# Attention of a gated block computed in two halves of 256 tokens through a state, and the zero rows stored later at the start

## The reference

```python
log_f = jax.nn.log_sigmoid(fg)
pcs = jnp.pad(jnp.cumsum(log_f, axis=-1), ((0, 0), (0, 0), (1, 0)))
mat = pcs[..., :, None] - pcs[..., None, :]
log_fg_matrix = jnp.where(ltr, mat[..., 1:, 1:], -jnp.inf)
log_D = log_fg_matrix + ig[..., None, :]
max_log_D = jnp.max(log_D, axis=-1, keepdims=True)
D = jnp.exp(log_D - max_log_D)
C = jnp.einsum('bhsd,bhtd->bhst', qh, kh) / math.sqrt(dh) * D
normalizer = jnp.maximum(jnp.abs(C.sum(axis=-1, keepdims=True)), jnp.exp(-max_log_D))
hst = jnp.einsum('bhst,bhtd->bhsd', C / (normalizer + eps), vh)
# heads normalised and scaled; x = x + tanh(g) * heads; then the experts on the normalised x
```

## Time and profile of the kernel before

| | us |
|---|---|
| median of three runs (lowest, highest) | 1904.91 (1904.54, 1905.46) |
| the profiled execution | 1903.81 |
| its span | 1902.1 |
| TensorE busy in the span | 1808.4 (95%) |
| VectorE busy | 1279.3 (67%) |
| ScalarE busy | 1100.7 (58%) |
| GpSimd busy | 689.4 (36%) |

### The profile page before, as it was taken

One profiled execution on the slowest core, in us unless ns is written; L12 is line 12 of the kernel. 1 busy time (PEld: TensorE's weight loads), 2 busy tenths in 40 slices (PEclk: granted clock), 3 DMA queues, 4 the chain that ended last, 5 costly groups with the idle time before them and its releaser, 6 DMA issues.

```text
span 1902.1 us, 29803 instructions
## 1 busy us (share of the span) xinstructions
PE 1808.4 (95%) x11068; PEld 1568.3 (82%) x11068; DVE 1279.3 (67%) x2890; ACT 1100.7 (58%) x2022; POOL 689.4 (36%) x507
## 2 busy tenths in 40 slices
PE   5999986699999999999999999999999999999997
PEld 3777765688888888888888888888888888888886
DVE  3799978786657665766576657665766576667551
ACT  3668667665555555555655565556555655565542
POOL 1101110425343533353435333533353435343333
PEclk8999987699999999999999999999999999999999
DMA  5364624525555555555555555555555555555544
GB/s 187 99 224 175 210 101 126 135 54 112 98 117 100 109 100 115 102 109 101 112 103 110 100 112 102 113 97 113 102 113 98 112 102 112 100 111 93 96 74 58
DMA packets 177777, 214.41 MB, mean 113 GB/s; under 512 B 20464, under 2 KB 102512, under 8 KB 176608
## 3 DMA queue, kind: packets, MB, share of 16 engines
q0 software_dynamic: 50176, 90.77, 31.4%
q1 hardware_dynamic: 127456, 121.74, 20.5%
HBM read 123.10 MB, written 89.34 MB: 112 GB/s over the span
## 4 chain that ended last, share of the span: by engine, by line
PE 85%; DVE 8%; ACT 3%; issue 2%; DMA 1%; SPq 1%; POOL 1%; POOLq 0%; DVEq 0%; ACTq 0%
PE PS L964 41%; PE PS L942 35%; PE PS L791 2%; PE PS L920 2%; PE PS L782 2%; DVE stats L1356 1%; PE PS L810 1%; DVE decay L1413 1%; PE PS L730 1%; DVE x_lo L1701 1%; DVE stats L1425 1%; DVE xn L1365 1%; DVE x_back L1468 1%; PE PS L744 1%; DVE heads L1463 1%
## 5 line engine op out<-in xcount | busy, mean ns | idle before, releaser
L644 POOL DMA_INDIRECT out_dram<-y_out,rows_now x288 | 484.0, 1681 | 813.0 <-ACT y_out L1272 734.8
L942 PE MATMUL PS<-x_hi,w_hi 128*128 128x270 f32 x1792 | 520.0, 290 | 6.2 <-DVE x_lo L1701 4.3
L942 PE MATMUL PS<-x_lo,w_hi 128*128 128x270 f32 x1792 | 516.5, 288 | 0.0
L942 PE MATMUL PS<-x_hi,w_lo 128*128 128x270 f32 x1792 | 516.2, 288 | 0.0
L964 PE MATMUL PS<-w_hi,h_hi 128*120 128x512 f32 x1152 | 458.0, 398 | 6.7 <-DVE h_lo L1708 6.7
L964 PE MATMUL PS<-w_lo,h_hi 128*120 128x512 f32 x1152 | 453.8, 394 | 0.0
L964 PE MATMUL PS<-w_hi,h_lo 128*120 128x512 f32 x1152 | 453.2, 393 | 0.0
L942 PEld LDWEIGHTS PS<-x_hi,w_hi 128*128 128x128 f32 x1792 | 339.3, 189 | 31.2 <-issue 4.6
L942 PEld LDWEIGHTS PS<-x_lo,w_hi 128*128 128x128 f32 x1792 | 340.2, 190 | 21.0
L942 PEld LDWEIGHTS PS<-x_hi,w_lo 128*128 128x128 f32 x1792 | 339.0, 189 | 0.0
L964 PEld LDWEIGHTS PS<-w_hi,h_lo 128*120 128x120 f32 x1152 | 208.9, 181 | 58.8
(11 more groups left out here) (194 smaller groups left out, 2283.2 us busy)
## 6 DMA issues: line engine op xcount, KB each, us to landing
w_raw<-in_L_ffn_W_dram SPq DMA_DIRECT2D x128, 256.0 KB, 4.0
w_raw<-in_L_ffn_W_dram SPq DMA_DIRECT2D x64, 512.0 KB, 4.5
x_front<-in_x_dram SPq DMA_DIRECT2D x8, 1024.0 KB, 7.0
vs<-in_ctx_dram SPq DMA_DIRECT2D x32, 256.0 KB, 4.9
maxima<-maxima_rows SPq DMA_DIRECT2D x8, 1024.0 KB, 4.6
x_back<-in_x_dram SPq DMA_DIRECT2D x8, 1024.0 KB, 8.8
out_dram<-x_back SPq DMA_DIRECT2D x8, 1024.0 KB, 6.8
xn_rows<-xn SPq DMA_DIRECT2D x8, 1024.0 KB, 7.5
```

The source lines that it names most:

```text
L644: G.indirect_dma_start(out=out[:, :], out_offset=bass.IndirectOffsetOnAxis(ap=rows_now[0:RT, u % HI:u % HI + 1], axis=0), in_=y_out[0:RT, ...
L942: ins = T.matmul(product_at(k, i), w[:, slot, a, kt * P:(kt + 1) * P], v[:, side, x, kt, :], start=(kt == 0 and n == 0), stop=(kt == 1 and ...
```

## The change

A batch is attended in two halves of 256 tokens. Inside a half it is as before: keys of the half, decay, mask, scores, weighing (block pairs of both halves in one instruction, 512 columns for the even and 256 for the odd key blocks). What the second half reads of the first goes through a state of 128 x 129 for each head: the values of the first half are weighed by exp(col[t] - max[255]) (`weight_logs` on VectorE, `exp_weights` on ScalarE, `weigh_values` on GpSimd), TensorE sums the products of keys and weighed values (`states`, two heads a call), ScalarE copies them (`copy_state`). The queries of the second half are faded by exp(max[255] - max[s]) (`exp_fade` on ScalarE, `fade_queries` on GpSimd) and multiplied with the state in `outputs`. Context is key and value at once, so the state needs no turned copy. On SyncE, `slot(-1)` is put before the stores of the zero rows. The core of the diff (semaphores and buffers left out):

```diff
@@ sync @@
             load_ctx(1)
+            slot(-1)
             sp.dma_start(xn_dram[TOK:TOK + P, :], zeros[:, :]).then_inc(xn_stored, 16)
...
-            for b in range(-1, B):
+            for b in range(0, B):
                 slot(b)
@@ gpsimd @@
+            def weigh_values(b):
+                pool.wait_ge(front_copied, at(b, 8, 8))
+                pool.wait_ge(w_made, at(b, 1, 1))
+                wait_past(pool, state_made, at(b, 2, 0))
+                for t in range(2):
+                    each = w_first[:, t, :].rearrange("p (h o) -> p h o", o=1).to_broadcast([P, NH, VW])
+                    ins = G.tensor_tensor(v_first[:, t, :, :], vs[b % CTX_BUFS][:, t, :, :], each, ALU.mult)
+                ins.then_inc(v_weighed, 1)
+            def fade_queries(b, r):
+                pool.wait_ge(fade_made, at(b, 2, r + 1))
+                wait_past(pool, head_summed, at(b, 4, 0))
+                mine = slice(2 * r, 2 * r + 2)
+                G.tensor_tensor(q_faded[:, mine, :], qT[b % 2][:, mine, HALF:S], fade[:, mine, :], ALU.mult).then_inc(q_scaled, 1)
             def slot(b):
-                if there(b):
-                    for h in range(NH):
-                        mask(b, h)
+                mask(b, 0)
+                weigh_values(b)
+                fade_queries(b, 0)
+                mask(b, 1)
+                mask(b, 2)
+                fade_queries(b, 1)
+                mask(b, 3)
@@ tensor @@
-                for place, t in enumerate(SCORE_ORDER):
-                    wait_past(pe, scored, at(b, 16, 4 * h + READ[place]))
-                    T.matmul(score_ps[t], kT[p][:, h, t * P:(t + 1) * P], qT[p][:, h, t * P:S],
-                             start=True, stop=True).then_inc(scores_made, 1)
+                for v in range(2):
+                    wait_past(pe, scored, at(b, 2 * NH, 2 * h + v - 1))
+                    for u in range(2):
+                        t = 2 * u + v
+                        ins = T.matmul(score_ps[v][:, u, :], kT[p][:, h, t * P:(t + 1) * P], qT[p][:, h, t * P:(u + 1) * HALF],
+                                       start=True, stop=True)
+                    ins.then_inc(scores_made, 1)
+            def states(b, r):
+                pe.wait_ge(v_weighed, at(b, 1, 1))
+                wait_past(pe, state_copied, at(b, 2, r))
+                for i in range(2):
+                    h = 2 * r + i
+                    for t in range(2):
+                        ins = T.matmul(state_ps[:, i, :], vs[b % CTX_BUFS][:, t, h, 0:DH], v_first[:, t, h, 0:DH + 1],
+                                       start=(t == 0), stop=(t == 1))
+                ins.then_inc(state_made, 1)
             def outputs(b, h):
...
-                for s in range(ST):
-                    pe.wait_ge(scored, at(b, 16, 4 * h + NEEDED[s]))
-                    for t in range(s + 1):
-                        ins = T.matmul(head_ps[:, s, 0:DH + 1], decay[h % 2][:, t, s * P:(s + 1) * P],
-                                       vs[p][:, t, h, 0:DH + 1], start=(t == 0), stop=(t == s))
+                for s in (0, 2, 1, 3):
+                    u, v = s // 2, s % 2
+                    pe.wait_ge(scored, at(b, 2 * NH, 2 * h + v + 1))
+                    T.matmul(head_ps[:, s, 0:DH + 1], mine[:, u, v * P:(v + 1) * P], values[:, 2 * u, h, 0:DH + 1],
+                             start=True, stop=(s == 0))
+                    if v == 1:
+                        ins = T.matmul(head_ps[:, s, 0:DH + 1], mine[:, u, HALF:HALF + P], values[:, s, h, 0:DH + 1],
+                                       start=False, stop=(u == 0))
+                    if u == 1:
+                        pe.wait_ge(q_scaled, at(b, 2, h // 2 + 1))
+                        pe.wait_ge(state_copied, at(b, 2, h // 2 + 1))
+                        ins = T.matmul(head_ps[:, s, 0:DH + 1], q_faded[:, h, v * P:(v + 1) * P], state[:, h, 0:DH + 1],
+                                       start=False, stop=True)
                 ins.then_inc(head_summed, 1)
...
                 when(front, turn_front, 6)
+                when(b, states, 0)
                 when(front, turn_front, 7)
...
                 when(b, outputs, 1)
+                when(b, states, 1)
@@ scalar @@
                 for t in range(ST):
-                    ins = A.activation(decay[h % 2][:, t, t * P:S], maxima[p][:, h, t * P:S], ACT.Exp,
-                                       bias=cols[p][:, t, h:h + 1], scale=-1.0)
+                    u, v = t // 2, t % 2
+                    place = decay_odd(h)[:, u, :] if v else decay_even(h)[:, u, :]
+                    ins = A.activation(place, maxima[p][:, h, t * P:(u + 1) * HALF], ACT.Exp, bias=cols[p][:, t, h:h + 1], scale=-1.0)
                 ins.then_inc(decay_made, 1)
+            def exp_weights(b):
+                act.wait_ge(w_logged, at(b, 1, 1))
+                wait_past(act, v_weighed, at(b, 1, 0))
+                A.activation(w_first[:, :, :], w_log[:, :, :], ACT.Exp).then_inc(w_made, 1)
+            def exp_fade(b, r):
+                wait_past(act, q_scaled, at(b, 2, r - 1))
+                for h in range(2 * r, 2 * r + 2):
+                    ins = A.activation(fade[:, h, :], maxima[b % 2][:, h, HALF:S], ACT.Exp, bias=maxima[b % 2][:, h, HALF - 1:HALF], scale=-1.0)
+                ins.then_inc(fade_made, 1)
+            def copy_state(b, r):
+                act.wait_ge(state_made, at(b, 2, r + 1))
+                wait_past(act, head_summed, at(b, 4, 0))
+                A.activation(state[:, 2 * r:2 * r + 2, 0:DH + 1], state_ps, ACT.Copy, scale=SCORE_SCALE).then_inc(state_copied, 1)
...
                 when(b, exponentials, 0)
+                when(b, exp_weights)
...
                 when(front, copy_front, 3)
+                when(b, exp_fade, 0)
                 when(front, copy_front, 4)
...
                 when(front, copy_front, 6)
+                when(b, copy_state, 0)
                 when(front, copy_front, 7)
...
                 when(b, copy_head, 0)
+                when(b, exp_fade, 1)
                 when(back, normalise_heads, 0)
...
                 when(b, copy_head, 1)
+                when(b, copy_state, 1)
                 when(last, copy_router)
@@ vector @@
+            def weight_logs(b):
+                p = b % 2
+                dve.wait_ge(maxima_in[p], at_own(b, 16, 16))
+                wait_past(dve, w_made, at(b, 1, 0))
+                top = maxima[p][:, :, HALF - 1:HALF].rearrange("p h o -> p o h").to_broadcast([P, 2, NH])
+                V.tensor_tensor(w_log[:, :, :], cols[p][:, 0:2, :], top, ALU.subtract).then_inc(w_logged, 1)
             def weigh(b, h):
                 dve.wait_ge(decay_masked, at(b, 4, h + 1))
-                for place, t in enumerate(SCORE_ORDER):
-                    dve.wait_ge(scores_made, at(b, 16, 4 * h + MADE[place]))
-                    d = decay[h % 2][:, t, t * P:S]
-                    V.scalar_tensor_tensor(d, score_ps[t], SCORE_SCALE, d, ALU.mult, ALU.mult).then_inc(scored, 1)
+                for v, d in enumerate((decay_even(h), decay_odd(h))):
+                    dve.wait_ge(scores_made, at(b, 2 * NH, 2 * h + v + 1))
+                    V.scalar_tensor_tensor(d, score_ps[v], SCORE_SCALE, d, ALU.mult, ALU.mult).then_inc(scored, 1)
...
                 ahead, front, back, last = b + 2, b + 1, b - 1, b - 2
+                when(b, weight_logs)
                 when(back, head_stats, LAST_STATS)
                 when(b, weigh, 0)
```

34 lines of the change are left out of this document (24 added, 10 removed).

## The result

The changed kernel takes **1912.51 us**, the median of six runs (1911.14 to 1914.57), beside 1904.80 (1904.50 to 1908.18) for the kernel before in the same comparison. The ratio is 1.0038 with a 95% interval of 1.0028 to 1.0048: 7.7 us **slower**. The forecast was 1900.1, the range 1888 to 1908; sign and range were both wrong.

A forecast was written before the change was run, and what follows sets the result against it. TensorE and VectorE were both nearly full, alternating in the chain of waits. Start -0.4, slot 0 -1.8, slots 1 to 5 -1.75, slot 6 -1.15, slot 7 +0.3: -4.8 us, so a median of 1900.1, range 1888 to 1908.

The forecast's parts named there:

- the slack: Slots 1 to 5, ahead of g_max: residual starts 0.7 us late, fitting into the gate logarithms' 0.82 before TensorE's sums.
- The start: Up to the first exponentials: gate rows gain 2.9 to 4.3 us, maxima lose 2.7 to 5.5; taken as -0.4.
- the relief of VectorE: Behind g_max in a steady slot: only the weighing of head 3 changes, saving 0.6 us.
- contention: Slots 1 to 6: GpSimd's second faded-query product meets VectorE's residual and gate steps, charged 0.25 us a slot.
- the second rival: Gate steps, slots 1 to 5: GpSimd's products hold VectorE their whole length, +5.0 us (1905.2) or +9.2 (1909.3); chance 0.12.
- The first rival: TensorE idles more and its clock drops in slots 3 to 6: +6.2 us, 1906.3; chance 0.16.
- A wait was costed at nothing: ScalarE, slots 2 to 5: exp_weights waits for w_log with only copies queued behind it; cost taken as nothing.
- Slot 7: Hangs on ScalarE's normalisation: fades and state copy add 0.9 us, weighing saves 0.6, so +0.3.
- Slot 0: TensorE's matmuls one after another: heads 2 and 3 save 2.6 us, wait for first state costs 0.8, so -1.8.
- Slot 1: Same as a steady slot: 0.6 us saved less 0.25, so -0.35.
- slot 6: TensorE ends the wait at the sums: -0.55 us there and -0.6 behind g_max, so -1.15.
- The third rival: ScalarE's additions are covered and VectorE's relief counts in full: -16.3 us in all, 1888.6; chance 0.20.

The follow-up runs named there:

- e5: Changed kernel with GpSimd's products cut to 2 and 4 columns a head, part of the result left out: 1903.84 us, ratio 0.9992.
- e3: Changed kernel with GpSimd's second faded-query product moved ahead of the mask of head 2: 1908.52 us, ratio 1.0009.
- e2: Changed kernel with SyncE's slot(-1) put back behind the zero rows, so the halves alone: 1913.37 us, ratio 1.0037.
- e14: Changed kernel with ScalarE's one-hot rows ahead of exp_weights in slot 7: 1910.09 us, ratio 1.0022.
- e1: Kernel before with only SyncE's slot(-1) moved ahead of the zero rows: 1907.16 us, ratio 1.0006.
- e4: Changed kernel with four matmuls without a reader added on TensorE in each of slots 2 to 7: 1910.48 us, ratio 1.0019.
- e13: Changed kernel with products, fades and statistics reordered, TensorE fillers, early w_log except batch 7, early copies in slot 0, one-hot rows first in slot 7: 1899.15 us, ratio 0.9962.
- e12: Kernel before with matmuls without a reader on TensorE in slots 2 to 7 and ahead of the last turn: 1908.93 us, ratio 1.0015.

## Why the prediction was wrong, point by point

**Right**, with what it rested on. The prices of TensorE and VectorE: scores of a head 1.31 us, outputs 1.78 to 1.98, states 0.89 a call, weighing 0.93. GpSimd's products: 1.06 on the mean for the weighed values and 1.26 for a faded-query product with VectorE elsewhere, against 1.26. The Trainium skill (GPSIMD Engine Reference, section 3.1) made an estimated 1.1 of 520 columns; the trace agrees, with 1.06. `states` hardly waits for GpSimd (0.3 us in all ahead of its products, 0.7 ahead of their weight loads), and the residual does wait for ScalarE, 0.65 at the place named. With the products' length taken away (e5) the residual starts 13.14 behind the first transposes, 0.73 later than the 12.41 of before (forecast 0.7), and g_max comes 6.33 behind that instead of 6.98: the slack takes the delay in, as the sum had it.

**Right by luck.** The start, -0.42 against -0.4: with the same edit the first exponentials begin anywhere from 42.01 to 45.36.

**Behind g_max the relief of VectorE was 0.34 a slot, not 0.6.** The sum without its 0.25 of contention makes a steady slot 31.60; e5 has 31.94. From g_max to the next slot's first transposes it takes 12.47, and the kernel before 12.81. Weighing did shrink on the chain, from 1.59 to 0.93, but the normalisation of the rows behind (`second_norm`) grew. GpSimd's first mask of the next slot comes sooner, behind shorter exponentials, and now runs inside it (e5 has 2.23 to 2.24 there too); slot 5 of the changed kernel, then of the kernel before:

```profile
238.87 2.23 DVE L1450 TENSOR_SCALAR xn<-x_back,small 128x512 f32<-128x512 f32 x4
...
240.07 0.74 POOL L625 TENSOR_SCALAR_AFFINE_SELECT decay<-decay 128x512 f32<-128x512 f32 x1 [8.49 <-ACT decay L1114]
```

```profile
233.60 1.92 DVE L1365 TENSOR_SCALAR xn<-x_back,small 128x512 f32<-128x512 f32 x4
...
235.24 0.77 POOL L611 TENSOR_SCALAR_AFFINE_SELECT decay<-decay 128x512 f32<-128x512 f32 x1 [9.60 <-ACT decay L1052]
```

The mask started 0.28 before the normalisation's end and now starts 1.03 before it. That it is the mask which costs the 0.31 was not tested by a run.

**The contention was mis-sized.** The step that failed most charged 0.25 for GpSimd's second faded-query product meeting VectorE's residual and gate steps, from a stretch of 0.41 in two instructions of 512 columns, less the slack. What it met was a step of 16 columns, and that waited until the product was done: g_t took 1.02 instead of 0.17. Moving that product is worth 0.77 a slot (e3), cutting the length of all four 1.15 (e5), each against the 33.09 of slot 3. Such a loss of a whole product is the second rival, which had put 1.26 or 2.08 and a chance of 0.12. Taking the 0.41 of the two stretched rows as the size of any meeting was the error; the rows say only by how much those two instructions grew. The prediction's own range, 1897 to 1904, did not even hold its bounds: the start's +3.0 and a whole product of 1.26 in five slots (+5.0) make 1908. The Trainium skill (SBUF - State Buffer, "Who interferes with whom") has a VectorE instruction with two SBUF inputs and a GpSimd instruction that reads SBUF exclude each other for the whole instruction. The trace agrees: g_t, which has two, ends at 225.73 and the product at 225.70.

**The clock was put off as unlikely.** The first rival had the dips behind L868 in slots 3 to 6, at 1.54 each, with a chance of 0.16. In the profile they came in slots 4 to 6 (slot 2 dips in both kernels), at 0.95 where it can be read; in the traces of e2 and e14, with the same steps, they came behind L868 in slots 2 and 6. "A steady stretch keeps the full clock" was an argument from the kernel before; the gap ahead of L868 that the change adds, named in the same paragraph, was reason enough to doubt it.

**A wait was costed at nothing from steady slots alone.** For `exp_weights` the prediction named what is queued behind it, but only as slots 2 to 5 have it. Slot 7 has the one-hot rows there. Forecast +0.3, measured +1.64; with the queue mended (e14) slot 7 is 1.04 shorter than before, so the wait cost 2.68.

**Slot 0.** The savings were summed as if TensorE ran without a gap. It waits for the maxima with nothing left to do, and can start its matmuls at the lower clock: e1 shows it without the halves, 1.0 longer (27.98 instead of 26.97). That the shorter scores of head 0 leave more such idle time is argued, not shown. Forecast -1.8, measured -0.47, and +0.36 to +0.81 in e2, e4 and e14, which run the same steps there. Slot 1 (+1.84 instead of -0.35) has the same contention and, in the table of stretches, a clock of 0.5 from 90 to 96 us; how much of it is either was not measured by itself. Nor was slot 6 (+0.05 instead of -1.15) taken apart; the fillers of e4 bring it to 36.53, 0.85 under the kernel before, so much of that miss is the clock.

**The rivals were taken for exclusive.** Each was priced alone against a forecast that kept everything else. The first (with smaller dips) and the second sit on different engines and happened together, and the queue in slot 7, which no rival named, came on top; that is how the time came out above the range. The third rival, in which ScalarE's additions are covered and VectorE's relief counts, holds in part: with the same operations in another order, and fillers, the kernel takes 1899.15 (e13), where that rival had 1888.6. So the changed kernel lost to the order, not to the work. How much of e13's 7.1 under the kernel before is the halves' stays open: the fillers alone do not help that kernel (e12), but the other order of VectorE's statistics and the earlier copies in slot 0 were not tried on it.

## What to carry to other kernels

When an operation is put on an engine that shares something with the bottleneck, list the small steps of the bottleneck's chain that can meet it, and charge each the whole of the new operation, not the stretch that two long instructions showed. For every new wait, read the queue behind it in each kind of slot, the last ones too, and give a moved or added step the place in which the bottleneck is busy with something it does not disturb. Rivals on different engines add up: sum the ones that can hold at once before setting the range.
